# The down product of a mixture-of-experts phase: one full-precision product, or three rounded ones

## The reference, cut to what matters

```python
combine = (jax.nn.one_hot(tki, E, dtype=tkw.dtype) * tkw[..., None]).sum(1)
g = jax.nn.silu(jnp.einsum('th,eih->tei', h, w_gate))
u = jnp.einsum('th,eih->tei', h, w_up)
routed = jnp.einsum('tei,ehi->th', g * u * combine[:, :, None], w_down)
sg = jax.nn.silu(h @ sh_gate.T)
shared = sg * (h @ sh_up.T) @ sh_down.T
return (routed + shared).reshape(B, S, Hd)
```

## Time and profile before

| | |
|---|---|
| median of 3 runs | 845.33 us (843.93 to 845.87) |
| the profiled execution | 845.92 us |
| its span on the core | 844.1 us |
| TensorE | busy 817.3 us, 97% of the span |
| granted TensorE clock, mean | 0.993 of full speed |
| last mixture of experts | about 678 to 840 us of the span |

### The profile page before, as it was taken

How to read it: one execution, slowest core, us unless ns; L and a number is a source line. 1 busy time by engine, 2 the same in 40 slices (tenths; PEclk the granted TensorE clock), 3 DMA queues, 4 the chain that set the end, 5 groups by cost and what they waited for, 6 DMA issues and landing times.

```text
span 844.1 us, 13575 instructions
## 1 busy us (share of the span) xinstructions
PE 817.3 (97%) x4427; PEld 557.7 (66%) x4427; DVE 480.2 (57%) x1411; ACT 424.4 (50%) x778; POOL 447.4 (53%) x429
## 2 busy tenths in 40 slices
PE   4999999999999999999999999999999999999998
PEld 4876676777667666665766666656566576666664
DVE  6766636393846555335556757576756746545332
ACT  1434555656555343334667676756556562424231
POOL 5375656466654546376454444353555357565453
PEclk9799999999999999999999999999999999999999
DMA  9213030214422141441334131312123051424251
GB/s 313 86 49 101 1 101 1 99 65 158 133 82 87 56 145 53 142 124 35 80 94 113 42 98 36 104 42 61 48 54 86 23 156 62 155 62 149 73 153 47
DMA packets 44870, 75.29 MB, mean 89 GB/s; under 512 B 8992, under 2 KB 9632, under 8 KB 44672
## 3 DMA queue, kind: packets, MB, share of 16 engines
q1 hardware_dynamic: 44656, 74.42, 29.9%
q10 hardware_dynamic: 144, 0.01, 0.0%
HBM read 56.11 MB, written 1.51 MB: 68 GB/s over the span
## 4 chain that ended last, share of the span: by engine, by line
PE 89%; DVE 5%; ACT 3%; issue 2%; DMA 1%; SPq 0%; ACTq 0%; DVEq 0%
PE Y L945 21%; PE B L872 11%; PE B L870 11%; PE B L871 11%; PE B L1537 5%; PE B L1556 4%; PE B L1518 3%; PE B L1524 3%; PE B L1517 2%; PE T L1339 2%; PE Y L1406 2%; PE T L962 1%; DVE mxh L1818 1%; PE Y L1460 1%; DMA CT<-in_ctx_t 1%
## 5 line engine op out<-in xcount | busy, mean ns | idle before, releaser
L1213 POOL TENSOR_TENSOR shared<-shared,bcs 128x512 f32<-128x512 f32 x192 | 248.0, 1297 | 213.5 <-DVE shared L1249 189.6
L1249 DVE TENSOR_TENSOR shared<-shared,B 128x512 f32<-128x512 f32 x204 | 139.7, 686 | 221.6 <-PE B L872 184.1
L1085 ACT ACTIVATE shared<-B 128x512 f32<-128x512 f32 x204 | 121.8, 599 | 252.2 <-PE B L872 251.4
L945 PE MATMUL Y<-shared,down_lo 128*128 128x512 f32 x408 | 207.5, 594 | 0.0
L1758 POOL TENSOR_TENSOR shared_r<-shared_r,const 128x512 fp32r<-128x512 f32 (+1 forms) x128 | 115.7, 936 | 82.8 <-PE B L1518 52.2
L1818 DVE TENSOR_REDUCE mxh<-B 128x4 fp32r<-128x512 f32 (+1 forms) x128 | 78.9, 618 | 83.0 <-PE B L1518 82.2
L1685 ACT ACTIVATE shared<-B 128x512 f32<-128x512 f32 (+1 forms) x128 | 69.7, 544 | 49.9 <-PE B L1524 48.3
L1695 ACT COPY shared<-B 128x512 f32<-128x512 f32 (+1 forms) x128 | 64.7, 506 | 57.2 <-PE B L1537 57.1
L945 PEld LDWEIGHTS Y<-shared,down_lo 128*128 128x128 f32 x408 | 72.5, 190 | 21.4 <-issue 9.5
L870 PE MATMUL B<-shared_r,gate_hi 128*128 128x512 f32 x102 | 81.0, 794 | 0.0
L870 PE MATMUL B<-x_lo_r,gate_hi 128*128 128x512 f32 x102 | 75.6, 741 | 0.0
(11 more groups left out here) (317 smaller groups left out, 1426.8 us busy)
## 6 DMA issues: line engine op xcount, KB each, us to landing
bcs<-wrow SPq DMA_DIRECT2D x96, 256.0 KB, 3.8
shared_r<-shared_r SPq DMA_DIRECT2D x256, 64.0 KB, 2.0
bcs<-wrow SPq DMA_DIRECT2D x128, 128.0 KB, 3.1
gate_lo<-in_moe SPq DMA_DIRECT2D x9, 256.0 KB, 5.3
up_lo<-in_moe SPq DMA_DIRECT2D x9, 256.0 KB, 6.3
down_lo<-in_moe SPq DMA_DIRECT2D x9, 256.0 KB, 3.6
small<-in_small SPq DMA_DIRECT2D x1, 1372.5 KB, 10.6
X<-in_x SPq DMA_DIRECT2D x4, 256.0 KB, 5.1
```

Of the source, the lines that this page charges most:

```text
L945: nc.tensor.matmul(Y[:], w_raw[2][:, at:at + P], hid[(n0 + c) % HIDDEN], start=(i == 0), stop=(i == m["NC"] - 1))\
L1085: nc.scalar.activation(sg[(n0 + n) % ACTIVE], B[n % GATES][:], ACT.Silu).then_inc(sem("sg_ready"), 1)
L1213: gp.tensor_tensor(hid[(n0 + n) % HIDDEN], hid[(n0 + n) % HIDDEN], bcs[(PLACE.k0[p] + r // m["PER"]) % BROADCAST], ALU.mult)\
L1249: nc.vector.tensor_tensor(hid[(n0 + n) % HIDDEN], sg[(n0 + n) % ACTIVE], up[:], ALU.mult)\
```

## The change

It concerns phase 7 alone, and there chunks 5 to 16 of groups 1, 2 and 3: 36 chunks, called split here (`run.split`, which numbers them from 1).

- Their down product is made in three rounded parts instead of one unrounded product (`stream_down`).
- For this the down weights of chunks 5 to 16 are split while groups 0 and 1 run: ScalarE copies three pieces of 512 columns to `down_hi` at n = 9, 11 and 13, GpSimd makes the rest at n = 18, 22 and 26, in place of the unrounded weights.
- The hidden values have to be split as well. GpSimd now weights `sg` in place, before the multiplication; VectorE multiplies it by the up bank and leaves the result in that bank; ScalarE copies it, rounded, to `hid_hi` (`high`), behind silu of the next chunk; VectorE subtracts this copy from the bank into `hid_low` (`low`), in front of the multiplication of the next chunk.
- The up banks are four instead of three in this stream. The bank of a split chunk is free when `low` is done.
- The result of the previous group is copied out of `Y` at chunk 7, between silu and the high part's copy, instead of at chunk 8 in front of silu.

```diff
--- before.py
+++ after.py
@@ -312,6 +312,16 @@
             for k in range(2):
                 weights_lo(pool, nc.gpsimd, p, q, k, f"w_lo{p}")
 
+
+        WHOLE, HIGHS = 5, 10
+        late = Area()
+        down_hi = late.at_tile(15, [P, (MOE[7]["NC"] - WHOLE) * P], shared_r)
+        hid_hi = [late.at_tile(18 + i, [P, TG], shared_r) for i in range(HIGHS)]
+
+        def down_piece(q):
+
+            a, b = PIECES[7][q]
+            return slice((a - WHOLE) * P, (b - WHOLE) * P)
 
         area0 = Area()
         xhat0, sm = ([area0.tile([P, TG]) for g in range(NG)] for _ in range(2))
@@ -556,7 +566,9 @@
         area1 = Area()
         sg = [area1.tile([P, TG]) for i in range(ACTIVE)]
         bcs = [sb(f"bcs{i}", [P, TG])[:] for i in range(BROADCAST)]
+        hid_at = area1.at
         hid = [area1.tile([P, TG]) for i in range(HIDDEN)]
+        hid_low = [shared_r[:, hid_at + i * TG:hid_at + (i + 1) * TG] for i in range(HIDDEN)]
         x_hi0, x_hi0_r = two_views("x_hi0", [P, TG])
         x_lo0, x_lo0_r = two_views("x_lo0", [P, TG])
         x_hi = [x_hi0_r[:], area1.tile([P, TG], shared_r)]
@@ -704,6 +716,12 @@
                     self.first.append(len(self.chunks))
                     self.chunks += [(G, i) for i in range(MOE[p]["NC"])]
                 self.n0 = PLACE.n0[phases[0]]
+                self.ups = UPS if ride else UPS + 1
+                self.split = {}
+                for n, (G, i) in enumerate(self.chunks):
+                    p, g = self.groups[G]
+                    if p == 7 and g > 0 and i >= WHOLE:
+                        self.split[n] = len(self.split) + 1
                 end = len(self.groups) - 1
                 for G, (p, g) in enumerate(self.groups):
                     NC = MOE[p]["NC"]
@@ -727,6 +745,10 @@
                             for d, steps in table.items():
                                 for what in steps:
                                     self.ride.setdefault((engine, u + d), []).append((g, what))
+
+            def upper(self, n):
+
+                return B[GATES + n % self.ups]
 
             def hook(self, what, n):
                 return self.at.get((what, n))
@@ -937,6 +959,18 @@
             for q, (a, _) in enumerate(PIECES[p]):
                 if (p, g, i) == (3, 0, a):
                     pe.wait_ge(sem(f"raw_down3_{q}"), 16)
+            if c in run.split:
+                for q, (a, _) in enumerate(PIECES[p]):
+                    if (g, i) == (1, a):
+                        pe.wait_ge(sem("down_lo_ready"), q)
+                at, w = i * P, (i - WHOLE) * P
+                hi, lo = hid_hi[run.split[c] % HIGHS], hid_low[(n0 + c) % HIDDEN]
+                pe.wait_ge(sem("hid_lo_ready"), run.split[c])
+                nc.tensor.matmul(Y[:], down_hi[:, w:w + P], lo, start=False, stop=False)
+                nc.tensor.matmul(Y[:], down_hi[:, w:w + P], hi, start=False, stop=False)
+                nc.tensor.matmul(Y[:], w_lo[2][:, at:at + P], hi, start=False, stop=(i == m["NC"] - 1))\
+                    .then_inc(sem("down_mm") if i < m["NC"] - 1 else sem("y_ready"), 1)
+                return
             if i < m["SHARED"]:
                 pe.wait_ge(sem("product_ready"), n0 + c + 1)
             else:
@@ -994,11 +1028,13 @@
                         pe.wait_ge(sem("sg_ready"), n0 + n - GATES + 1)
                     product(B[n % GATES][:], 0, slice(at, at + P), x_hi[g % 2], x_lo[g % 2])\
                         .then_inc(sem("gated_mm"), 1)
-                    if n >= UPS:
-                        pe.wait_ge(sem("product_ready"), n0 + n - UPS + 1)
+                    if n - run.ups in run.split:
+                        pe.wait_ge(sem("hid_lo_ready"), run.split[n - run.ups])
+                    elif n >= run.ups:
+                        pe.wait_ge(sem("product_ready"), n0 + n - run.ups + 1)
                     elif p == 1 and n == 2:
                         pe.wait_ge(sem("p0_updated"), 2)
-                    product(B[GATES + n % UPS][:], 1, slice(at, at + P), x_hi[g % 2], x_lo[g % 2])\
+                    product(run.upper(n)[:], 1, slice(at, at + P), x_hi[g % 2], x_lo[g % 2])\
                         .then_inc(sem("upper_mm"), 1)
                     if (p, n) == (1, 2):
                         turn(1, 0)
@@ -1075,14 +1111,32 @@
                 if GB - 1 in js:
                     ins.then_inc(sem("xhat_ready"), 1)
 
+            def high(n):
+                act.wait_ge(sem("product_ready"), n0 + n + 1)
+                k = run.split[n]
+                if k > HIGHS:
+                    freed = next(c for c in run.split if run.split[c] == k - HIGHS)
+                    H, i = run.chunks[freed]
+                    after_down(act, *run.groups[H], i)
+                nc.scalar.copy(hid_hi[k % HIGHS], run.upper(n)[:]).then_inc(sem("hid_hi_ready"), 1)
+
             for n, (G, i) in enumerate(run.chunks):
                 p, g = run.groups[G]
-                if i == LAG and G > 0:
+                if i == LAG and G > 0 and n - 2 not in run.split:
                     result_act(act, run.groups[G - 1][0], run.step(G) - 1)
                 act.wait_ge(sem("gated_mm"), n0 + n + 1)
                 if n >= ACTIVE:
                     act.wait_ge(sem("product_ready"), n0 + n - ACTIVE + 1)
                 nc.scalar.activation(sg[(n0 + n) % ACTIVE], B[n % GATES][:], ACT.Silu).then_inc(sem("sg_ready"), 1)
+                if i == LAG - 1 and n - 1 in run.split:
+                    result_act(act, run.groups[G - 1][0], run.step(G) - 1)
+                if n - 1 in run.split:
+                    high(n - 1)
+                if p == 7 and n in DOWN_ACT:
+                    q = DOWN_ACT[n]
+                    act.wait_ge(sem(f"raw1_{q}"), 96)
+                    nc.scalar.copy(down_hi[:, down_piece(q)], w_raw[2][:, piece(7, q)])\
+                        .then_inc(sem("down_hi_ready"), 1)
                 if (p, n) == (1, 1):
                     turned_act(act, 1)
                 elif (p, n) == (7, 4):
@@ -1115,6 +1169,8 @@
                     ride_act(act, g, what)
                 if run is STREAMS[0] and n in SPLIT_ACT:
                     weights_hi(act, 3, *SPLIT_ACT[n])
+            if len(run.chunks) - 1 in run.split:
+                high(len(run.chunks) - 1)
             if run is STREAMS[1]:
                 act.wait_ge(sem("y_ready"), LAST)
                 act.wait_ge(sem("yt_ready"), LAST - 1)
@@ -1124,6 +1180,8 @@
                                          scale=tgate[:, 7:8]).then_inc(sem("last_ysb"), 1)
 
         SPLIT_ACT = {57: (0, 0), 58: (0, 1), 62: (1, 0), 63: (1, 1), 66: (2, 0), 67: (2, 1), 69: (3, 0), 70: (3, 1)}
+        DOWN_ACT = {9: 1, 11: 2, 13: 3}
+        DOWN_POOL = {18: 1, 22: 2, 26: 3}
         SPLIT_POOL = {n + 1: qk for n, qk in SPLIT_ACT.items()}
 
         LOADED = {}
@@ -1209,10 +1267,22 @@
                     r = g * m["NR"] + i - m["SHARED"]
                     loaded, count = tile_loaded(p, r // m["PER"])
                     pool.wait_ge(loaded, count)
-                    pool.wait_ge(sem("product_ready"), n0 + n + 1)
-                    gp.tensor_tensor(hid[(n0 + n) % HIDDEN], hid[(n0 + n) % HIDDEN],
+                    if n in run.split:
+                        pool.wait_ge(sem("sg_ready"), n0 + n + 1)
+                        by_weight = sg[(n0 + n) % ACTIVE]
+                    else:
+                        pool.wait_ge(sem("product_ready"), n0 + n + 1)
+                        by_weight = hid[(n0 + n) % HIDDEN]
+                    gp.tensor_tensor(by_weight, by_weight,
                                      bcs[(PLACE.k0[p] + r // m["PER"]) % BROADCAST], ALU.mult)\
                         .then_inc(sem("weighted"), 1)
+                if p == 7 and n in DOWN_POOL:
+                    q = DOWN_POOL[n]
+                    c = piece(7, q)
+                    pool.wait_ge(sem("down_hi_ready"), q)
+                    after_down(pool, 7, 0, PIECES[7][q][1] - 1)
+                    gp.tensor_tensor(w_lo[2][:, c], w_raw[2][:, c], down_hi[:, down_piece(q)].bitcast(F32),
+                                     ALU.subtract).then_inc(sem("down_lo_ready"), 1)
                 H = run.hook("stats", n - 1)
                 if H is not None and run.step(H) + 2 < LAST:
                     power(run.step(H) + 2)
@@ -1236,18 +1306,35 @@
             else:
                 pieces = iter(())
             setup = setup_dve(dve, st)
+
+            def low(n):
+                dve.wait_ge(sem("hid_hi_ready"), run.split[n])
+                H, i = run.chunks[n - HIDDEN]
+                after_down(dve, *run.groups[H], i)
+                nc.vector.tensor_tensor(hid_low[(n0 + n) % HIDDEN], run.upper(n)[:],
+                                        hid_hi[run.split[n] % HIGHS].bitcast(F32), ALU.subtract)\
+                    .then_inc(sem("hid_lo_ready"), 1)
+
             for n, (G, i) in enumerate(run.chunks):
                 p, g = run.groups[G]
                 if i == 0:
```

(26 more changed lines are left out.)

## The result

The changed kernel took 841.22 us (median of 20 executions, 837.65 to 846.51), the kernel before, on the same chips, 847.11 (20 executions, 842.57 to 850.13). The ratio is 0.9937, 95% interval 0.9921 to 0.9954: 0.63% faster, 3.9 to 6.7 us. On the 845.33 us of the table ahead that gives 840.0; the forecast was 840.1, and faster. The interval is 2.8 us wide, so that the two lie 0.1 apart is luck.

A forecast was written before the change was run, and what follows sets the result against it. TensorE's issued products were taken to bound the last phase: -5.8 us gain + 0.6 stall = -5.2, from 845.92 to 840.7, median 840.1. Forecast range 838.9 to 841.7 (0.64); 8 in 10: 838.3 to 844.5.

The forecast's parts named there:

- TensorE's gain: 36 split chunks: three rounded products replace one down product, 0.16 us less each, 5.8 us, at most 6.1.
- The ring: VectorE and ScalarE in split chunks: multiplication, copy, subtraction, next multiplication take 1.96 us, within TensorE's 2.10 per chunk.
- The slow ring: Rival: VectorE-ScalarE loop takes 2.26 us, gain gone, 845.2 us; chance 0.11 for no change, 0.14 for 841.7 to 843.6.
- The stall of 0.6 us in group 1: TensorE waits for a silu about chunks 12 to 14, as peak delay exceeds the room by 0.6 us.
- lateness: Delay of VectorE's multiplications in group 1, added up chunk by chunk, peaking at 4.3 us.
- slack: How late a multiplication may be before TensorE's gate product four chunks on waits for silu: 3.7 us.
- the table: Group 1's chunk-by-chunk sum of multiplication delays against a 2.10 us pace, chunks 5 to 11, peak 4.3 us.
- Which path is tight: The gate product's wait for silu binds first, 3.7 us of room; the fourth up bank's own path has 4.2.
- The interference: VectorE and GpSimd block each other: four VectorE operations each wait up to 1.30 us; 849.6 us, chance 0.08.
- the slower rival: VectorE and GpSimd get in each other's way, 5.2 us more delay a group: 849.6 us, chance 0.08.
- The late turn of weights: `w_row` copied behind chunk 15's high copy, up to 3 us later in groups 1 and 2: nothing, or 1 us.
- the copy of `Y` at chunk 7: Moved ScalarE copy, done before TensorE needs it 1.40 us after the last down product: costs nothing.

The follow-up runs named there:

- again: The changed kernel once more, unaltered, against the kernel before: ratio 0.9940, 841.2 us; last phase, first silu to last copy out of `Y`, 155.42 us.
- pe_alone: Kernel before, with three rounded products of other data for each of the 36 down products and no splitting of values or weights: ratio 0.9924, 839.99 us.
- copy_twice: Changed kernel with the high copy made twice, first into an unread tile: ratio 1.0049 to the kernel before, 849.31 us.
- ring_alone: Changed kernel with all copies and subtractions, but one unrounded down product of the high parts: ratio 1.0008 to the kernel before, 846.95 us.
- three_banks: Changed kernel with three up banks in the last phase instead of four: ratio 0.9945 to the kernel before, 840.53 us.
- first trace: The first profiled execution of the changed kernel, nothing altered: 846.51 us; last phase, first silu to last copy out of `Y`, 156.69 us.
- late_row: Changed kernel with SyncE storing `w_row` twice, one store behind the other, before the read back: ratio 0.9965 to the kernel before, 843.91 us.
- late_row_first: Changed kernel with `w_row` stored twice and its copy put in front of the high copy of chunk 15: ratio 0.9938 to the kernel before, 840.33 us.
- result_back: Changed kernel with the copy of `Y` back at chunk 8, in front of silu: ratio 0.9958 to the kernel before, 842.27 us.
- group0_row: Changed kernel with chunks 10 to 16 of group 0 split too and `w_row` copied before the high copy: ratio 0.9916 to the kernel before, 839.36 us.
- row_first: Changed kernel with the copy of `w_row` back in front of the high copy of chunk 15: ratio 0.9936 to the kernel before, 841.65 us.

## Why the prediction was right, and where it wasn't

**TensorE's gain: right, sized 0.3 too low.** I took 36 x 0.16 = 5.8 and named 6.1 as the most; it is 6.1 to 6.2 (again, pe_alone). The chunk is 2.08 us, not 2.10: the difference of two rounded durations is worth less than one start-to-start time.

**The ring: right.** 1.96 forecast, 1.95 measured; both steps between VectorE and ScalarE at about 0.03, writing PSUM for nothing, copy 0.59, subtraction 0.69. The slow ring is refuted. copy_twice shows a term that its price lacked, since I had group 3 pay nothing: a ring slower than TensorE catches up only in the five whole chunks, and at the end of group 3 nothing covers its lateness. No run has the ring of 2.26 that I priced. ring_alone shows that the other added work (weight pieces, ScalarE's and VectorE's time) is hidden.

**The stall of 0.6 us in group 1: this step failed.** No such stall came. In both traces of the change, silu of chunk 14 ends 0.4 us before TensorE wants the gate product of chunk 16. Of the step's two sizes, lateness and slack, each was off by half a microsecond. TensorE's timeline of `again`, the gate products of chunks 12 and 16:

```profile
741.25 0.79 PE L892 MATMUL B<-shared_r,gate_hi 128*128 128x512 f32 x1
741.88 0.39 PE L893 MATMUL B<-shared_r,gate_hi 128*128 128x512 f32 x1
...
750.57 0.40 PE L892 MATMUL B<-shared_r,gate_hi 128*128 128x512 f32 x1
750.81 0.39 PE L893 MATMUL B<-shared_r,gate_hi 128*128 128x512 f32 x1
```

*Lateness: 3.8, not 4.3.* The multiplication of chunk 12 starts at 748.39, 6.51 behind 741.88; in the last chunk it is 2.73. My 4.3 lies near this only because two errors of the table stood against each other. A split chunk pays off only when its down product is issued, `LAG` = 8 chunks later, in group 1 from chunk 13 on. Until then TensorE's chunk is 2.25 us and not 2.10, and over the seven chunks from 5 to 12 that makes 1.0 us less lateness. The other way, VectorE needs 19.97 us from the multiplication of 5 to that of 12 (728.42 to 748.39), where the table has 19.39: chunks 7 and 10 are 0.7 shorter each than I had them and chunks 5, 6, 8 and 9 together 0.8 longer, but chunk 11, for which I counted no work of VectorE, takes 3.25 and not 2.10.

*Slack: 4.2, not 3.7.* The two gate products are 750.81 - 741.88 = 8.93 apart, not 8.40. Of the 0.53 more, 0.45 is the turn of the tokens' weights on TensorE at chunk 15 (L1003), which my sum left out, and the rest is the last unrounded down product. 4.2 less 3.8 is the 0.4 us of room. In group 2 the room behind a split chunk is never under 2.1 on this path.

**Which path is tight: wrong.** I wrote that the up bank isn't the one that stalls. I had priced it as if VectorE did nothing between multiplication and subtraction (the same work of chunk 11 that the table lacks). In chunk 11 it does, on VectorE's timeline of `again`:

```profile
745.14 0.69 DVE L1328 TENSOR_TENSOR B<-shared,B 128x512 f32<-128x512 f32 x1
745.74 1.41 DVE L631 SCALAR_TENSOR_TENSOR comb<-w,rec 128x128 f32<-128x128 f32 x1
747.07 0.67 DVE L256 TENSOR_TENSOR X<-X,T 128x512 f32<-128x512 f32 x1
747.78 0.69 DVE L1314 TENSOR_TENSOR shared_r<-B,shared_r 128x512 fp32r<-128x512 f32 x1
```

The subtraction ends at 748.47, the up product of chunk 15, which takes the same bank, starts at 748.75: 0.28 of room, less than the 0.38 of the silu path. With three banks it would be 1.80 late, and three_banks shows 1.97 of stall.

**The interference: there, hidden in `again`, not in the first trace.** L631 took 0.28 before and 1.41 here, beside a multiplication of GpSimd from 745.71 to 747.00. In group 2 of the first trace three operations are of the same kind. VectorE's timeline, each beside a multiplication of GpSimd (774.96 to 776.26, 776.73 to 778.03, 789.19 to 790.49):

```profile
775.37 1.04 DVE L665 TENSOR_TENSOR s<-sig,small 128x128 f32<-128x128 f32 x1
776.44 1.66 DVE L670 TENSOR_TENSOR pair<-s 128x96 f32<-128x96 f32 x3
...
789.25 1.26 DVE L626 TENSOR_SCALAR tot<-tot 128x4 f32<-128x4 f32 x1
```

In group 2 of `again` they take 0.28, 0.52 and 0.17, 3.0 us less. The first two stand in front of the subtraction of chunk 5, for whose bank the up product of 9 waits, and the third in front of that of chunk 10, for whose bank the up product of 14 waits. So the 1.3 us of stall hang on these waits as well as on the late weights. late_row has still later weights and the third operation at 1.26, but the first two at 0.75 and 0.52, and none of these stalls; it had lost its 1.91 before. No run separates the two causes, so what each would cost alone is open. That is the mechanism of the slower rival, at one to three waits a group and not the four full ones that it needs. All 36 subtractions and 36 multiplications with an operand in PSUM stay at 0.69, though GpSimd works through half of the time. By the Trainium skill (SBUF — State Buffer, Who interferes with whom) VectorE and GpSimd lock each other out over a shared port pair, for operations with both inputs in SBUF or in the two-port modes alone; both halves of that agree with these rows.

**The late turn of weights: real, but not always.** I priced it at 0 or 1 us; together with the interference it was 1.3 in the first trace and 0 in `again`, with the same kernel. What makes the weights late is how far behind the write the next transfer is issued. In 5 of the 14 traces of this case (first trace, late_row, late_row_first, result_back, group0_row) that is 3.2 to 3.6 us in group 2, in all the others, and in groups 1 and 3 always, 1.6 to 1.8. With the copy of `w_row` in row_first's place such a wait did no harm in the one trace that has both (group0_row: 3.6, two of the routing operations at 1.63 and 1.25 as well, and no stall in group 2); in the change's place it went with 1.3. That is the one part of the change that I would take back, though no trace of row_first itself had the long gap. late_row shows a way to TensorE that I missed: by the copy of `Y` at chunk 7, which I priced at nothing. Why the write takes longer at times is open; no run was made for it.

So two errors of the sum stood against each other, which is luck: 0.3 too little gained, 0.6 too much paid. On L the forecast is 0.9 too long against `again` and 0.4 too short against the first trace.

## What to carry to other kernels

Work that replaces an operation issued `LAG` chunks later is paid for at once and pays back `LAG` chunks later: count lateness and slack against the pace that holds in each chunk, not against the new pace, and put every engine's other work of those chunks into the table. A ring over two engines that is shorter than the chunk of the engine that bounds costs nothing while the spare banks and buffers cover its peaks (1.95 against 2.08 here, nothing in `again`, 1.3 in the first trace); the longer one that was tried, 2.43, cost 8.6 us, more than the 6.1 gained. When two traces of one kernel differ, look at both for every wait before you name one cause. Where the profiled execution had a stretch at a lower clock, compare a stretch of the same work with the same clock, not the spans.

## What the runs showed that I had not expected

The step from writing 32 rows to DRAM to issuing the next transfer was 1.6 to 1.8 us nearly always, and 3.2 to 3.6 in one group of 5 traces of 14; two traces of the same kernel, one with it and one without, differ by 1.3 us at the end. `comb`, 0.28 us for 128 columns, took 1.41 beside GpSimd, five times as long. The mean granted clock of two 20 us stretches was 0.83 in one execution and 1.00 in the other, with the same instructions; over the executions of the changed kernel a mean clock of 0.998 goes with 837.65 us and 0.985 with 845.73.
